# A vision tower on one Trainium2 core: the class query's weighted values as a 257th column of each quad of heads

## The reference, cut to what matters

```python
b, s, d = src.shape
dh = d // H
qkv = src @ in_proj_w.T + in_proj_b
q, k, v = jnp.split(qkv, 3, axis=-1)
...
scores = jnp.einsum('bhqd,bhkd->bhqk', q, k) / math.sqrt(dh)
attn = jax.nn.softmax(scores, axis=-1)
ctx = jnp.einsum('bhqk,bhkd->bhqd', attn, v)
ctx = ctx.transpose(0, 2, 1, 3).reshape(b, s, d)
dense_output = ctx @ out_proj_w.T + out_proj_b
```

## Time and profile before

| | |
|---|---|
| time, median of 3 runs | 1315.51 us (1312.16 to 1318.94) |
| span of the profiled execution | 1336.2 us, mean granted clock 0.865 |
| TensorE busy (matmul) | 1107.7 us, 83% |
| VectorE, ScalarE, GpSimd busy | 58%, 29%, 35% |
| second attention, its eight images | about 547 to 1000 us of the span |
| one image in the steady state | 53.6 to 56.0 us |

### The profile page before, as it was taken

How to read it: one execution, slowest core, us unless ns; L and a number is a source line. 1 busy time by engine, 2 the same in 40 slices (tenths; PEclk the granted TensorE clock), 3 DMA queues, 4 the chain that set the end, 5 groups by cost and what they waited for, 6 DMA issues and landing times. The chain is left out here.

```text
span 1336.2 us, 22077 instructions
## 1 busy us (share of the span) xinstructions
PE 1107.7 (83%) x6752; PEld 794.3 (59%) x6752; DVE 777.3 (58%) x1867; ACT 385.0 (29%) x951; POOL 465.6 (35%) x576
## 2 busy tenths in 40 slices
PE   0267898859999945889999999999888999689898
PEld 0265776656677722546556566565548998455555
DVE  8965666544222223656565665755633776588885
ACT  0242333112222221223343333432314443222221
POOL 4952000352000025122223222220115776376665
PEclk9978999659999977667696886968778999799999
DMA  9908000222212116245162551523204000000000
GB/s 315 306 1 284 1 0 0 76 101 70 63 56 64 57 35 119 54 83 100 41 121 59 96 113 43 105 76 48 82 20 150 0 0 0 1 9 8 16 16 17
DMA packets 66432, 93.81 MB, mean 70 GB/s; under 512 B 9153, under 2 KB 58761, under 8 KB 65201
## 3 DMA queue, kind: packets, MB, share of 16 engines
q1 hardware_dynamic: 63152, 84.42, 23.9%
q0 software_dynamic: 3200, 8.43, 2.0%
HBM read 52.23 MB, written 40.33 MB: 69 GB/s over the span
## 5 line engine op out<-in xcount | busy, mean ns | idle before, releaser
L2247 DVE TENSOR_REDUCE fa_nm<-fa_ps 128x2 f32<-128x514 f32 x128 | 82.9, 689 | 87.1 <-PE fa_ps L2489 85.1
L1499 PE MATMUL ex_ps<-we_raw,ex_xT 128*128 x320 | 117.9, 492 | 0.0
L2040 ACT ACTIVATE fa_eT<-fa_ps 128x512 f32<-128x512 f32 x128 | 73.4, 590 | 75.7 <-PE fa_ps L2542 74.3
L3290 PE MATMUL qf_ps<-qf_wg,qf_xT 128*128 128x352 f32 x272 | 90.0, 480 | 2.1 <-ACT qf_xT L3131 1.4
L2489 PE MATMUL fa_ps<-fa_ks,fa_qs 64*128 64x258 f32 x256 | 74.1, 423 | 19.7 <-DMA fa_ks<-fa_qk_rows 15.2
L451 PE MATMUL tk_ps<-tk_u,tk_qb 64*32 64x64 f32 x1024 | 24.8, 274 | 69.5 <-POOLq L318 56.7
L2489 PEld LDWEIGHTS fa_ps<-fa_ks,fa_qs 64*128 64x128 f32 x256 | 53.5, 273 | 45.4 <-issue 29.5
L1413 DVE COPY ex_hT<-ex_ps 128x384 f32<-128x384 f32 x40 | 22.3, 558 | 95.3 <-PE ex_ps L1508 91.5
L2542 PE MATMUL fa_ps<-fa_qs,fa_ks 66*128 66x256 f32 x256 | 71.9, 375 | 6.9 <-ACT fa_eT L2040 6.9
L3290 PEld LDWEIGHTS qf_ps<-qf_wg,qf_xT 128*128 128x128 f32 x272 | 50.7, 195 | 37.3 <-issue 6.6
L1499 PEld LDWEIGHTS ex_ps<-we_raw,ex_xT 128*128 128x128 f32 x320 | 55.5, 193 | 22.4 <-issue 1.5
(11 more groups left out here) (491 smaller groups left out, 2475.1 us busy)
## 6 DMA issues: line engine op xcount, KB each, us to landing
x_rows<-tk_zero SPq DMA_DIRECT2D x8, 2176.0 KB, 17.4
we_raw<-in_L_ffn_W SPq DMA_DIRECT2D x24, 384.0 KB, 7.8
fa_qs<-fa_qk_rows SPq DMA_DIRECT2D x16, 514.0 KB, 8.1
fa_ks<-fa_qk_rows SPq DMA_DIRECT2D x32, 257.0 KB, 10.2
ex_xin<-x_rows SPq DMA_DIRECT2D x40, 128.0 KB
y_rows<-ex_y SPq DMA_DIRECT2D x40, 128.0 KB, 1.7
fa_rsb<-fa_rs_rows SPq DMA_DIRECT2D x32, 132.0 KB, 2.9
fa_qk_rows<-fa_qhl SPq DMA_DIRECT2D x32, 128.5 KB
```

The source lines that it names most:

```text
L1499: last = mm(ps[:, bank + t % 2, 0:HD], xT[:, t % 2, k, :], raw[:, ds(e, 1), m, k * HD:(k + 1) * HD], start=(k == 0), stop=(k == KC - 1))
L2040: cp(eT[:, j % 8, :], ps[:, ST + j % 2, :], ACT.Exp).then_inc(z["e_ready"], 1)
L2247: nc.vector.tensor_reduce(nm[:, :, j], ps[:, b:b + 2, 0:TOK], AX.X, ALU.max, negate=True).then_inc(z["max_done"], 1)
L3290: last = mm(ps[:, GB + 2 * g + a, 0:HALF], xT[:, k, :], wg[:, g, k, a * HALF:(a + 1) * HALF], start=(k == 0), stop=(k == KC - 1))
```

## The change

The class query becomes column 256 of every quad. The product with `vblk` takes 257 columns, and eight products of one column with `pcT` stand between it and the eight products of 256 columns. `class_context` and `take_class` go, with the semaphores `clsq_ps` and `clsq_taken`. `take_quad` copies 257 columns. All quads use columns 0 to 256 of the bank. `quad` for c = 0 waits for `pt_taken`, and what waited for `clsq_ps` (GpSimd's `class_values`, ScalarE's `values` and `class_probs`, for the buffers of two images before) waits for the last `quad_ps` of that image.

```diff
@@ sums_out, on SP
             def sums_out(u, p):
-                sp.wait_ge(z["clsq_taken"], u + 1)
                 sp.wait_ge(z["cx_taken"], QUADS * (u + 1))
@@ class_values on GpSimd; the same in values and class_probs on ScalarE
                 if not isinstance(u, int) or u >= 2:
-                    pool.wait_ge(z["clsq_ps"], u - 1)
+                    pool.wait_ge(z["quad_ps"], QUADS * (u - 1))
@@ take_quad, on ScalarE
-                cp(cx[:, p, c, 0:SEQ], ps[:, CB, (c % 2) * SEQ:(c % 2 + 1) * SEQ], ACT.Copy).then_inc(z["cx_taken"], 1)
-
-            def take_class(u, p):
-                act.wait_ge(z["clsq_ps"], u + 1)
-                cp(cx[:, p, :, SEQ:TOK], ps[:, CB, 0:QUADS].unsqueeze(2), ACT.Copy).then_inc(z["clsq_taken"], 1)
+                cp(cx[:, p, c, 0:TOK], ps[:, CB, 0:TOK], ACT.Copy).then_inc(z["cx_taken"], 1)
@@ ScalarE's body
                     sparse_probs(u + 1)
-                take_class(u, p)
                 turned_class_weights(u)
@@ quad, on TensorE
                     pe.wait_ge(z["vblk_ready"], u + 1)
-                    if not isinstance(u, int) or u:
-                        pe.wait_ge(z["clsq_taken"], u)
+                    pe.wait_ge(z["pt_taken"], u + 1)
                 if not (isinstance(u, int) and u == 0 and c == 0):
                     pe.wait_ge(z["cx_taken"], QUADS * u + c)
-                cols = slice((c % 2) * SEQ, (c % 2 + 1) * SEQ)
-                mm(ps[:, CB, cols], vblk[:, p, 4 * c:4 * c + 4, :], e0T[:, p, 0:SEQ], start=True, stop=False)
+                mm(ps[:, CB, 0:TOK], vblk[:, p, 4 * c:4 * c + 4, :], e0T[:, p, :], start=True, stop=False)
                 for k in range(2):
                     for j in range(4):
-                        last = mm(ps[STRIP * j:STRIP * (j + 1), CB, cols], v[:, p, k, 4 * c + j, :],
-                                  eT[:, (4 * c + j) % 8, k * SEQ:(k + 1) * SEQ], start=False, stop=(k == 1))
+                        out, i = ps[STRIP * j:STRIP * (j + 1), CB, :], 4 * c + j
+                        mm(out[:, SEQ:TOK], v[:, p, k, i, :], pcT[:, p, k, i:i + 1], start=False, stop=False)
+                for k in range(2):
+                    for j in range(4):
+                        out, i = ps[STRIP * j:STRIP * (j + 1), CB, :], 4 * c + j
+                        last = mm(out[:, 0:SEQ], v[:, p, k, i, :], eT[:, i % 8, k * SEQ:(k + 1) * SEQ], start=False,
+                                  stop=(k == 1))
                 last.then_inc(z["quad_ps"], 1)
-
-            def class_context(u, p):
-                pe.wait_ge(z["cx_taken"], QUADS * u + 4)
-                pe.wait_ge(z["pt_taken"], u + 1)
-                for c in range(QUADS):
-                    mm(ps[:, CB, c:c + 1], vblk[:, p, 4 * c:4 * c + 4, :], e0T[:, p, SEQ:TOK], start=True, stop=False)
-                    for k in range(2):
-                        for j in range(4):
-                            last = mm(ps[STRIP * j:STRIP * (j + 1), CB, c:c + 1], v[:, p, k, 4 * c + j, :],
-                                      pcT[:, p, k, 4 * c + j:4 * c + j + 1], start=False, stop=(k == 1))
-                last.then_inc(z["clsq_ps"], 1)
@@ TensorE's body
                     if sl == 15:
-                        class_context(u, p)
                         turn_class_weights(u)
```

More of the change, by code:

```diff
@@ L1630, in fused_attention @@
              "pt_taken", "s2_ps", "m2_ready", "e2_ready", "wk_done", "wk_ready", "wt_ps", "wt_taken", "wc_ps", "wc_taken", "ck_ps",
-             "e0_ready", "st_ps", "e_ready", "quad_ps", "cx_taken", "clsq_ps", "clsq_taken", "sm_out", "sm_in", "rs_ready", "rs_out",
+             "e0_ready", "st_ps", "e_ready", "quad_ps", "cx_taken", "sm_out", "sm_in", "rs_ready", "rs_out",
              "rsb_in", "cn_ready", "cc_ready", "proj_ps", "z_added", "fetched", "s2c_in", "m2c_ready", "e2c_ready", "wkc_ready",
@@ L2001, in values @@
                 if t == 0 and (not isinstance(u, int) or u >= 2):
-                    act.wait_ge(z["clsq_ps"], u - 1)
+                    act.wait_ge(z["quad_ps"], QUADS * (u - 1))
                 act.wait_ge(z["v_ps"], 2 * u + t + 1)
```

## The result

| | before | changed |
|---|---|---|
| median of the runs beside each other | 1317.22 us (1312.16 to 1321.13) | 1306.65 us (1303.52 to 1308.50) |
| ratio | 1 | 0.9908, 95% interval 0.9885 to 0.9932 |
| span of the profiled execution | 1336.2 us | 1305.9 us |
| TensorE products recorded | 6752 | 6688 |

The changed kernel is 0.9% faster. A second measurement of the same pair gave 1307.47 against 1319.11 us, ratio 0.9924 (0.9898 to 0.9949). The forecast was 1305.6 us. The two profiled spans differ by 30 us, and that isn't the change: the second attention begins 12.6 us earlier in the new profile (the first sparse scores at 532.43 instead of 545.01 us), 13.0 us lie in the second attention, and the rest behind it.

What follows compares the result with a forecast made beforehand. TensorE's order of work was taken to bound steady images. Removing the class group (−2.52 us an image) less added columns (+1.32) and 1.0 at the end summed to −10.1, scaled −9.9: 1305.6 us, range 1298 to 1314.

Steps and rivals of the forecast that it cites:

- The path: Steady images of the second attention: the order of work on TensorE sets the end, unless a wait takes its place.
- What goes, 2.52 us an image: Slots 14 to 16: removing the 3.34 us class group gains 2.52; some 0.8 becomes a new wait of head 11.
- what follows keeps its pace: After head 11: `turn_maxima` waits no longer than before, and heads 12 to 15 alternate with VectorE as before.
- What comes, 0.33 us a quad: Each quad's eight one-column products cost 0.33 us, as in the class group; 1.32 us an image.
- 20 ns a record: One-column products: this looks like an instruction's cost, not that of columns, so 0.33 us a quad was kept.
- The lower bound of 0.17: Quads at the high clock: if the one-column group follows the clock, 0.17 us a quad, giving 1301.5 us.
- the sign of being wrong: Profile after: wrong if quads had grown by less than 0.17 or more than 0.51 us.
- Its rival: Thin quad products and head 11's wait lengthen the 1.2 GHz stretch, 2.0 us an image; 1319.3 us, slower; chance 0.07.
- The sum: Whole kernel: first image −1.86, next six −7.2, last −1.0; −10.1 us of the span, scaled −9.9.
- +0.66: First image: quads of slots 4 and 7 cost 0.66 us, taken in by TensorE's slot 9 wait for VectorE.
- What was hidden: First image's wait for VectorE takes in 0.66 us; last image's `project` wait for GpSimd, 1.59 us, takes in quad 0.
- The end of the stage: Last image: without the class group TensorE turns VectorE's weights at about 977.1 instead of 978.08, gaining 1.0 us.

Runs made afterwards that it cites:

- e1: Changed kernel without the 32 one-column products of an image, against the kernel before: 1300.3 us, ratio 0.9878.
- e9: Changed kernel with the class column inside `eT` and the turn of the first maxima before head 11, against the kernel before: 1301.63 us, ratio 0.9870.
- e12: The changed kernel once more, unaltered, against the kernel before: 1307.47 us, ratio 0.9924.
- e4: Changed kernel with VectorE copying the class probabilities into column 257 of `eT`'s halves, no one-column products, against the kernel before: 1301.27 us, ratio 0.9881.
- e11: Changed kernel with column in `eT`, turn before head 11 and 11 extra dense products an image, against the kernel before: 1285.86 us, ratio 0.9740.

## Why the prediction was right, point by point

**The path.** TensorE's order sets the end of a steady image: held. By the terms below its list lost 2.32 us an image and gained 0.63, together 1.7; the fast kind of image went from 54.0 to 52.2 us, 1.8, the slow kind from 55.9 to 54.8, only 1.1. Why the slow kind gained less isn't explained.

**What goes, 2.52 us an image.** Nearly. From the sparse scores' start to head 11 it is now 3.97 us (634.12 to 638.09), as the prologue's 3.92 said. But to the turn of the rows it is 8.14 us; before it was 10.46, from 709.54 to 720.00. So 2.32, not 2.52: head 11 starts 0.05 us later than the prologue said, and from head 11 to the turn of the rows it is 4.17 us instead of 4.02. The step "what follows keeps its pace" was the one that was a little off.

**What comes, 0.33 us a quad.** The term that was mis-sized. It is 0.13 at the high clock, with the group's own 0.14 confirmed by the tripled products, and 0.22 to 0.24 at the low one; so about 0.63 an image instead of 1.32. The price was taken from the class group, where only the low clock was seen and where every group of eight stands between two products of 128 partitions. The argument that 20 ns a record looks like the cost of an instruction was wrong: in the quads a record costs 9 ns. The lower bound of 0.17, halving with the clock, was the better guess. This is also the sign of being wrong that the prediction named and that came true: three quads of four grew by less than 0.17 us. The price was wrong, and the range held because it allowed for other prices. The rule cited from the Trainium skill (TensorEngine Tiling (Array Packing), Instruction Overhead: about 60 cycles for a matmul) would have made it 0.40 us at the high clock, as an estimate; this trace disagrees, at 0.14, for products on 32 output partitions. The prediction also read the 0.51 us of the class group's `vblk` products as agreeing with a drain at the change of mode. The row doesn't show that: PE's loader is busy for 0.49 of these 0.51 us, so the loads alone can account for them.

**The clock.** Its rival was given 0.07 and priced at +2.0 us for an image that turns slow. Of the mechanism a part came true: four of six images in one profile and three of six in the other were slow, against two of six before, at 2.6 us each over the fast kind. One profile of the kernel before and two of the changed one are too few to count kinds, but the runs say the same in another way. In the second measurement the mean clock is 0.8694 over ten runs of the changed kernel and 0.8704 over the fifteen of the kernel before beside them. As a mean clock of 0.87 means 26% of the time at the low level, both spend about 342 us at 1.2 GHz, though some 16 us of low-clock work left the program. So other work runs at the low clock in its place. How much that costs is an estimate. At the low clock the same work takes about twice as long (the wide group of a quad 1.84 us against 0.98). If all the low time that left came back with other work, the 16 us would be worth 8, and the sum below would give about 6 us; if none did, 13.1. The runs gave 10.6 and 11.6, between the two.

**The sum, with the terms as measured.** 7 × −2.32 + 19 × 0.13 + 7 × 0.24 − 1.0 = −13.1 us of path. The runs gave −10.6 and −11.6. The difference of about 2 us would be less than one more slow image of 2.6 us; no run shows that it is that. The forecast's −9.9 came near because the price of the columns was too high by about 4 us and the removal and the clock were too kind by about 3: the path was understood, the closeness of the number is luck.

**The stretch ahead of the images.** From the start of the first sparse scores to the end of the next image's it is now 51.45 us, before 56.65: 5.2 less, where the sum had +0.66. Up to the end of TensorE's wait for VectorE in slot 9 the two kernels take nearly the same time, 34.87 us now and 35.03 before, so the quads of slots 4 and 7 were taken in, as forecast. The rest, up to the end of the next sparse scores, differs by 5.0 us, and in its clock:

```profile
580.04:601.66 21.62, 21.26 (x78) 12.33 (x78) 9.31 (x21) 5.20 (x11) 7.20 (x12) 0.50 0.12 38
...
567.30:583.88 16.58, 15.92 (x110) 9.35 (x110) 9.31 (x21) 4.99 (x11) 7.21 (x12) 0.77 0.22 58
```

The first row is the kernel before, at 1.2 GHz all through; the second the changed one, at 0.77. Less work isn't the reason, since no class group stood in this stretch. Nor is it shown to be the change: from end to end of the sparse scores the stretch takes 54.7 us at 0.69 in e1 and 54.6 at 0.69 in e9, like the kernel before, but 49.0 at 0.74 in e12 and 48.6 at 0.75 in e4, though all four have the change. So within this pair of profiles the clock gave 5 us here and took some in the images. A single pair of profiles doesn't price the change; the ratio of the runs does.

**What was hidden.** In the last image `project` waited for GpSimd, and the first image's quads lay before a wait for VectorE; from the end of the last class group's place to GpSimd's first step of the next stage it is now 66.6 us (907.74 to 974.36), before 70.3 (929.65 to 999.93): −3.7, where 2.52 + 1.0 were expected. The six images between the two stretches went from 54.65 to 53.97 us in the mean, and to 53.5 in the changed kernel's second profile, where 53.4 was expected.

**The end of the stage**, to the earlier trace rows (2601 was 2615, 2608 was 2622, 2595 was 2609):

```profile
953.04 0.34 DVE L2326 TENSOR_SCALAR fa_got<-fa_got,fa_r2c 8x257 f32<-8x257 f32 x1
953.50 0.38 PE L2601 MATMUL fa_ps<-ident,fa_got 8*128 8x8 f32 x2 [2.72 <-DVEq L2328]
...
954.38 9.04 PE L2608 MATMUL fa_ps<-fa_qs,fa_wcm 128*8 128x256 f32 x32 [0.51 <-DVEq L2334]
...
961.66 2.35 POOL L1898 TENSOR_TENSOR fa_cx<-fa_cx,fa_rsb 128x1028 f32<-128x1028 f32 x1 [17.63 <-DMA fa_rsb<-fa_rs_rows]
...
965.56 1.99 PE L2595 MATMUL fa_ps<-wf_o,fa_cx 128*128 128x256 f32 x8
```

TensorE is ready first and waits 2.72 us for VectorE's weights; it turns them 0.12 us after they end. That is the overlap that the prediction named.

## What to carry to other kernels

When a group of small products leaves TensorE's list, look at which wait its time had been hiding, and take the distance from a place in the same trace where the group doesn't stand (here the prologue, right to 0.05 us for head 11 and to 0.2 for what follows). Price a small product by the start of what follows it, at the clock at which it will run. And before counting a gain of a few microseconds on TensorE, cut the trace into repeats of the loop and write the granted clock beside each: if they come in kinds, the clock can be worth more than the edit.

## What the runs showed of the hardware

- **Added work made the kernel faster.** Three dense products an image shortened the low-clock stretch from 17.1 to 23.9 us to 10.2 or 13.6, and the image from 52.2 or 54.8 us to 51.0. The place decides: the same kind of product behind the fall gave 58 us.
- **The clock fell with and without a wait before it.** The Trainium skill says, in TensorE: Matmul & The Clock Gate, part 1, that the clock follows how busy the engine is, and its section on HAM oscillation gives idle gaps as the cause. The one slow image of e11 goes with that: the clock fell within a wait of 2.05 us. In the changed kernel it fell 9.9 and 7.1 us after the last wait had ended, in slices in which TensorE was busy for 2.00 of 2.00 us, and three dense products ahead of that place did away with this fall.
- **The length of an image comes in kinds.** At a clock of 0.78 an image took about 54.8 us (changed), 54.7 (turn moved), 54.2 (column in `eT`) and 54.3 (no columns); at 0.83 it took 52.2 (changed), 51.4 (column in `eT`) and 51.1 (no columns). The step from one kind to the other, 2.6 to 3.2 us, is larger than each of these edits, so one image more of the slow kind hides a gain. Two images lay between the kinds: 52.1 us (no columns) and 52.6 (column and turn).
- One-column products on strips of 32 output partitions cost 9 ns a record at the high clock, and 15 (0.24 us for 16) at the low one in a quad, 20 in the class group.
